# A two-block attention and FFN kernel on one core: another order at the beginnings of three attention passes

## The reference

```
x = x + 0.5 * _L0_ffn_ref(_layernorm(x), ...)      # passes 0 and 1 (DEPTH = 2)
x = x + _L0_attn_ref(_layernorm(x), ...)           # causal linear attention
x = x + 0.5 * _L0_ffn_ref(_layernorm(x), ...)      # passes 2 and 3
x = x + 0.5 * _L1_ffn_ref(...); x = x + _L1_attn_ref(...); x = x + 0.5 * _L1_ffn_ref(...)

# one layer of _L0_ffn_ref
h = shift_token(x); q, k, v = split(h @ wqkv)      # 8 heads of 64
q, k = rotary_xpos(l2norm(q) * qs, l2norm(k) * ksc)
o = local_attention(q, k, v)                       # window 128, looks one block back
x = x + o @ wo
h = layernorm(shift_token(x)) * lg + lb
a, g = split(h @ w1 + b1); x = x + (a * gelu(g)) @ w2 + b2
```

## Time and profile before

| what | value |
|---|---|
| device time, median of 3 runs | 3074.22 us (3072.13 to 3074.41) |
| the profiled execution: its device time, its span | 3073.63 us, 3071.7 us |
| busy share of the span: PE, PE weight load, DVE, ACT, POOL | 95%, 83%, 76%, 57%, 54% |
| shares of the chain that ended last | PE 82%, DVE 7%, issue 4%, POOL 3% |
| mean granted TensorE clock | 0.989 of full speed |
| pass 0, 1 and 3: first attention transpose on PE | 19.06, 612.46 and 2019.63 us |
| second scores (slot 1) on PE | 52.56, 643.17 and 2051.91 us |

### The profile page before, as it was taken

One profiled execution on the slowest core, in us unless ns is written; L12 is line 12 of the kernel. 1 busy time (PEld: TensorE's weight loads), 2 busy tenths in 40 slices (PEclk: granted clock), 3 DMA queues, 4 the chain that ended last, 5 costly groups with the idle time before them and its releaser, 6 DMA issues.

```text
span 3071.7 us, 95309 instructions
## 1 busy us (share of the span) xinstructions
PE 2927.1 (95%) x34258; PEld 2561.2 (83%) x34258; DVE 2340.4 (76%) x6543; ACT 1745.9 (57%) x4596; POOL 1655.8 (54%) x1836
## 2 busy tenths in 40 slices
PE   6999989989999999998999989989999899999899
PEld 5888878878887888887888878878888788888788
DVE  6888777677777787877677777767777788777766
ACT  4777742267777224775777762257777422554345
POOL 7778830078886224334788851057888345227610
PEclk9999999999999999999999999999999999999999
DMA  4211121021111101000211121012111200100001
GB/s 141 71 45 45 45 82 31 24 62 43 42 39 39 44 20 43 12 11 26 64 42 39 39 87 32 24 32 69 41 40 44 62 21 7 28 1 1 1 15 41
DMA packets 178759, 122.62 MB, mean 40 GB/s; under 512 B 27532, under 2 KB 175336, under 8 KB 178024
## 3 DMA queue, kind: packets, MB, share of 16 engines
q1 hardware_dynamic: 177432, 117.77, 14.3%
q10 hardware_dynamic: 1104, 1.90, 0.2%
HBM read 48.29 MB, written 20.98 MB: 23 GB/s over the span
## 4 chain that ended last, share of the span: by engine, by line
PE 82%; DVE 7%; issue 4%; POOL 3%; DMA 1%; ACT 1%; SPq 1%; DVEq 0%; POOLq 0%; ACTq 0%
PE bank L377 7%; PE bank L379 7%; PE bank L378 7%; PE pair_bank L561 6%; PE scores L522 5%; PE scores L377 4%; PE scores L378 4%; PE scores L379 4%; PE bank L492 3%; PE pair_bank L377 2%; PE pair_bank L788 2%; PE pair_bank L787 2%; PE pair_bank L786 2%; PE scores L732 2%; PE scores L731 2%
## 5 line engine op out<-in xcount | busy, mean ns | idle before, releaser
L2736 POOL TENSOR_TENSOR prob<-prob,rsum 128x384 f32<-128x384 f32 x512 | 457.4, 922 | 254.6 <-DVE rsum L1925 254.6
L1261 ACT ACTIVATE prob<-prob,nmax 128x192 f32<-128x192 f32 x1024 | 452.1, 444 | 158.5 <-DVE nmax L1919 158.5
L1463 ACT ACTIVATE gate<-scores,bias 128x512 f32<-128x512 f32 x192 | 132.4, 690 | 511.9 <-PE scores L379 511.9
L2723 POOL TENSOR_TENSOR rn<-ss,mhalf 128x16 f32<-128x16 f32 x128 | 375.3, 2932 | 10.7
L2704 POOL TENSOR_TENSOR rstd<-meanvar,eps 128x4 f32<-128x4 f32 x48 | 11.0, 230 | 624.1 <-DVE meanvar L1850 624.1
L377 PE MATMUL bank<-wqkv_hi,hT_hi 128*128 128x512 f32 x768 | 335.1, 436 | 8.0 <-DVE hT_lo L1858 3.7
L2730 POOL TENSOR_TENSOR qk<-rot_t 128x512 f32<-128x512 f32 x256 | 322.6, 1280 | 19.4 <-DVE ss L1892 12.7
L1919 DVE CUSTOM_DVE_ANT_0 prob<-scores,masks,rn 128x192 f32<-128x192 f32 x768 | 267.5, 414 | 65.6 <-PE scores L522 65.2
L379 PE MATMUL bank<-wqkv_hi,hT_lo 128*128 128x512 f32 x768 | 305.2, 397 | 0.2 <-issue 0.2
L378 PE MATMUL bank<-wqkv_lo,hT_hi 128*128 128x512 f32 x768 | 303.1, 395 | 0.0
L1268 ACT ACTIVATE probT<-scores 128x384 f32<-128x384 f32 x512 | 225.3, 497 | 10.7 <-PE scores L540 10.7
(11 more groups left out here) (347 smaller groups left out, 9530.9 us busy)
## 6 DMA issues: line engine op xcount, KB each, us to landing
Vlo<-V SPq DMA_DIRECT2D x256, 64.0 KB, 2.0
Vhi<-V SPq DMA_DIRECT2D x256, 64.0 KB, 2.0
H<-Y SPq DMA_DIRECT2D x128, 64.0 KB, 1.8
H<-ya SPq DMA_DIRECT2D x128, 64.0 KB, 1.8
yb<-Y SPq DMA_DIRECT2D x128, 64.0 KB, 1.6
HB<-Y SPq DMA_DIRECT2D x32, 256.0 KB, 2.8
HB<-yb SPq DMA_DIRECT2D x32, 256.0 KB, 3.1
raw<-in_L_ffn_wqkv SPq DMA_DIRECT2D x4, 1536.0 KB
```

The costliest lines, as they stand in the source:

```text
L1261: e.activation(pb, pb, ACT.Exp, bias=nm[r][:, x:x + 1], scale=-1.0, accum_out=sums[r][:, x:x + 1]).then_inc(s_acEX[gi], 1)
L2723: e.tensor_tensor(rn[u][:, :], ss[u % 2][:, :], mhalf[:, :], ALU.pow).then_inc(s_plRN, 1)
L2736: e.tensor_tensor(pair, pair, rs[:, 2 * gi:2 * gi + 2].unsqueeze(2).to_broadcast([P, 2, KW]), ALU.mult).then_inc(s_plPN[gi], 1)
```

## The change

The change rewrites the beginning of passes 0, 1 and 3 and gives these passes a first slot with an order of its own (`first_slot`), on PE, ACT, DVE and POOL. Tile 2 is the third tile.

- PE: the transposes of tile 0's q move ahead of `v_(1, 1)`. The waits for POOL's preparations and for the FFN's last Y sums stand behind `v_(1, 1)` instead of ahead of `qk_(1, 1, 0)`. The k projection of tile 2 moves ahead of the transposes of tile 0. The q projection of tile 2 moves behind the first scores.
- ACT: the square of tile 2's q moves from before the first exponentials to behind them; the copies of the turned q of tile 0 and of v of tile 1 change places.
- DVE: the last Y sums (`finish`) move behind `norm_(0, 0, 1)`. The rotation and the sum of tile 2's q move behind the first scores. In the first slot they stand ahead of the second `rs_`, the rotation of tile 2's k and the low part of tile 3's input.
- POOL: in passes 1 and 3 `wo_weights` and the first mask move from ahead of tile 0's adds to behind them (pass 0 had them there). Tile 2's q add moves behind the four `pn_` of the first slot.

```diff
@@ PE, begin and the new first slot
                     ht(2, 2)
+                    qk_(1, 1, 0)
+                    qk_(2, 2, 1)
+                    tr_(0, 0, 1)
+                    tr_(0, 0, 0)
+                    v_(1, 1)
                     e.wait_ge(s_prepB, need['B'] + 4 + OFF)
                     if run:
                         e.wait_ge(s_dvYB, U * GRP * run + OFF)
-                    qk_(1, 1, 0)
-                    tr_(0, 0, 1)
-                    qk_(2, 2, 1)
-                    v_(1, 1)
-                    tr_(0, 0, 0)
+
+                def first_slot():
+                    sc_(0, 0)
+                    ht(3, 3)
                     qk_(2, 2, 0)
+                    v_(2, 2)
+                    pt_(0, 0, 0)
+                    pt_(0, 0, 1)
+                    tr_(1, 1, 0)
+                    qk_(3, 3, 0)
+                    tr_(1, 1, 1)
+                    pt_(0, 0, 2)
+                    pt_(0, 0, 3)
+                    qk_(3, 3, 1)
@@ ACT
                     tr_(0, 0, 1)
+                    tr_(0, 0, 0)
                     v_(1, 1)
-                    tr_(0, 0, 0)
+
+                def first_slot():
+                    qk_(2, 2, 1)
+                    sc_(0, 0, 0)
+                    sc_(0, 0, 1)
                     qk_(2, 2, 0)
+                    ht(3, 3)
+                    v_(2, 2)
+                    pt_(0, 0, 0)
+                    pt_(0, 0, 1)
+                    tr_(1, 1, 0)
+                    qk_(3, 3, 0)
...
@@ DVE
-                    if finish:
-                        finish()
                     qk_(1, 1, 1)
                     ht(2, 2)
                     norm_(0, 0, 1)
+                    if finish:
+                        finish()
                     sum_(1, 1, 1)
                     sum_(1, 1, 0)
                     qk_(1, 1, 0)
...
+                def first_slot():
+                    sc_(0, 0)
+                    rs_(0, 0, 0)
+                    norm_(1, 1, 1)
                     qk_(2, 2, 0)
+                    rs_(0, 0, 1)
+                    qk_(2, 2, 1)
+                    ht(3, 3)
                     sum_(2, 2, 0)
+                    sum_(2, 2, 1)
+                    qk_(3, 3, 0)
+                    sum_(3, 3, 0)
@@ POOL
                     e.memset(V[U - 1][:, :], 0.0).then_inc(s_prepB, 1)
-                    wo_weights()
...
-                if run:
+                if run == DEPTH:
                     mask_of(0)
...
                     add_(0, 0, 0)
-                    if run == 0:
-                        wo_weights()
-                        e.wait_ge(s_raw2, need['raw2'] + OFF)
-                        mask_of(0)
+                    wo_weights()
+                    e.wait_ge(s_raw2, need['raw2'] + OFF)
+                    mask_of(0)
...
+                def first_slot():
+                    add_(1, 1, 1)
+                    for gi in range(NG):
+                        pn_(0, 0, gi)
+                    add_(2, 2, 0)
+                    pow_(2, 2)
```

More of the change, by code:

```diff
@@ L669, in pass_A @@
                 for u in range(U):
-                    slot(u, u)
+                    if u == 0 and run != DEPTH:
+                        first_slot()
+                    else:
+                        slot(u, u)
                     if u < 2:
@@ L1357, in pass_A @@
                     begin()
-                slot(0, 0)
                 if run == DEPTH:
+                    slot(0, 0)
                     linear_tail['yn'](NT - 1)
+                else:
+                    first_slot()
                 for u in range(1, U):
@@ L2038, in pass_A @@
                     e.wait_ge(s_stb, 16 * GRP * ((run + 1) // 2) + OFF)
-                iteration(0)
+                for u in range(U):
+                    if u == 0 and run != DEPTH:
+                        first_slot()
+                    else:
+                        slot(u, u)
+                    extra(0, u)
                 with e.Fori(0, NIT - 2 if run else GRP - 4) as i:
```

## The result

The changed kernel takes 3084.05 us (median of 6 runs, 3082.59 to 3091.99) beside 3074.04 us for the kernel before on the same chip (6 runs, 3070.16 to 3076.29). The ratio is 1.004, 95% interval 1.0029 to 1.0052: slower by 10 us. The forecast was 3077.9 us with a range up to 3081.5, so the time lies outside it, on the slow side.

A forecast was written before the change was run, and what follows sets the result against it. PE's chain of waits (82%) was taken as the bound. Passes 1, 3 and 0 add 1.55 + 1.55 + 0.6 = 3.7 us: profiled 3073.63 becomes 3077.3, on the median 3077.9 us; range 3073.0 to 3081.5.

The forecast's parts named there:

- The order: Beginnings of passes 1, 3 and 0: the new instruction order lengthens them by 1.55, 1.55 and 0.6 us, 3.7 together.
- the held normalisation: DVE, tile 0's k, passes 1 and 3: POOL's add starts first and holds it, so the 1.58 us stays.
- the chain through DVE's rotation: Tile 0's q transposes wait for DVE's rotation of tile 1's q, ending at 628.77; first scores only 0.33 us earlier.
- the exposed table load: ACT ahead of the first exponentials: 0.69 us of the load shows, leaving 0.90 of 1.59 us gained.
- tile 3's q behind its low part: PE, first slot: this projection waits for DVE's low part of its input and comes 1.55 us later.
- The clock: PE in the beginnings: the forecast allowed a fall of the granted clock more or less, 3076 to 3080 us.
- rival 1: PE in the beginnings: clock falls twice in each, four more falls at 1.57 us, +10 us, 3084; chance 0.12.
- The price of a fall: PE in the beginnings: one fall to 1.2 GHz costs 1.57 us, read from pass 3 before.
- 2: DVE, passes 1 and 3: normalisation not held, all behind it 1.1 us earlier, +1.5 us, 3075.7; chance 0.13.
- 3: First slot stays as short as it was, only the earlier reading of scores counts: -5.0 us, 3069.2; chance 0.07.
- 4: ACT, passes 1 and 3: exposed table load costs more, +1.1 us together, sum 4.8 us, 3079.0; chance 0.08.

The follow-up runs named there:

- experiment 5: Changed kernel with 7 spare 32-bit matmuls a pass filling PE's waits ahead of tile 0's q transposes and in the first slot: 3086.89 us (one run).
- experiment 2: Kernel before with ten spare matmuls in PE's first-slot wait for the first probabilities, passes 0, 1 and 3: 3077.38 us, ratio 1.0006.
- experiment 1: Changed kernel with 22 spare 512-column matmuls a pass filling PE's waits ahead of tile 0's q transposes and in the first slot: 3084.77 us, ratio 1.0037.
- experiment 12: Changed kernel with four spare 32-bit matmuls only in the wait ahead of tile 0's q transposes, passes 1 and 3: 3079.77 us, ratio 1.002.
- experiment 3: Changed kernel with v of tile 1 back ahead of tile 0's q transposes on PE and ACT: 3080.62 us, ratio 1.0022.
- 4: Kernel before with only tile 2's q moved into the first slot, on all four engines: 3078.77 us, ratio 1.0008.
- 6: Changed kernel with DVE's last Y sums back ahead of the rotation of tile 1's k: 3073.04 us in a single run.
- 9: Changed kernel with POOL's tile 0 q add waiting for DVE's normalisation of tile 0's k, passes 1 and 3: 3081.81 us, ratio 1.0023.
- 7: Kernel before with only the Y sums moved behind the normalisation, and PE's wait for them behind the beginning: 3077.55 us (one run).
- experiment 8: Kernel before with POOL's tile 0 q add waiting for DVE's normalisation of tile 0's k, passes 1 and 3: 3073.6 us, ratio 0.9998.
- 10: Changed kernel with DVE's last Y sums back ahead of the rotation of tile 1's k, timed over ten runs: 3079.27 us, ratio 1.002.
- 11: Changed kernel with Y sums back in their old place and POOL's tile 0 q add behind DVE's normalisation, passes 1 and 3: 3079.79 us, ratio 1.0013.

## Why the prediction was wrong

**The order: right.** Spare matmuls take the clock out of the comparison. Without falls pass 1 costs +1.51 us (predicted 1.55): first scores 0.27 us earlier (0.33), slot 1.78 us longer. Pass 3 costs 32.22 - 30.69 = +1.53. In pass 0 I took +0.6. There DVE's layer norm sets when the scores are read: 21.34 us from the first transpose after, 21.35 in experiment 5 although its first scores come 1.6 us later. The readings, after first and experiment 5 (first transpose at 18.75) second:

```profile
40.71 0.42 DVE L1951 CUSTOM_DVE_ANT_0 prob<-scores,mask,rn 128x192 f32<-128x192 f32 x1 [0.16 <-issue]
40.10 0.42 DVE L1959 CUSTOM_DVE_ANT_0 prob<-scores,mask,rn 128x192 f32<-128x192 f32 x1 [0.19 <-PE scores L522]
```

So the pass is split at that reading. Without a fall it takes 33.34 us in the new order (experiment 5). In the old one it is an estimate: 23.03 us to the reading (before), and 9.39 from there to the second scores (experiment 2, no fall in that part), 32.42. That is +0.92. Together 3.96 us, where the forecast had 3.7. The reasons stood too: the held normalisation, the chain through DVE's rotation, the exposed table load (in experiment 1 it ends 0.69 us behind the first row minimum, as worked out), tile 3's q behind its low part. In experiment 12 it waits for just that (0.94 us for hT_lo); after, slow transposes put ACT's copy of the turned q last instead.

**The clock: the step that failed.** The prediction let the clock fall once more or less, and gave 0.12 to rival 1, two falls in each beginning. Its case against that rival was "pass 1 had 7.7 us of waits at a clock of 1.00". That sum did not carry over. In pass 1 before the longest wait was 2.55 us and other work stood between the waits; the prediction's own working had a single piece of 3.4 us ahead of tile 0's q transposes (3.33 measured), and three waits of about 1 us with only transposes between them in the slot. Both were followed by a fall in passes 1 and 3 each time that they were left unfilled, and in neither pass when they were filled. Over the profiles without spare matmuls in the slot, the new slot fell in passes 1 and 3 in all 16 cases (after, 3, 4, 6, 9 to 12), the old one in 2 of 6 (before, 7, 8). The result is three falls more than before, five for two.

**The price of a fall: too small.** 1.57 us was taken from the earlier trace rows, and is right for the old slot (1.59, experiment 2). The new ones are split where DVE first reads the scores, since the first fall also slows the scores themselves (2.30 us instead of 1.57). Counted from the first transpose, DVE reads them at 22.14 us in pass 1 and 21.92 in pass 3, and at 19.79 and 19.78 in experiment 1: the first fall costs 2.35 and 2.14 us. From that reading to the second scores it takes 14.34 and 14.42 us, and 12.43 and 12.44 in experiment 1: the second costs 1.91 and 1.98. In pass 0 it costs 35.28 - 33.34 = 1.94. The price is not fixed: in experiment 12 the same fall in the slot cost 2.80 us in pass 1 and 1.57 in pass 3.

**The sum.** Falls after: 2.35 + 1.91 + 2.14 + 1.98 + 1.94 = 10.32 us. Falls before: 1.59 in pass 3 and 33.50 - 32.42 = 1.08 in pass 0, 2.67 us. The difference of 7.65 and the order's 3.96 are the 11.6 us of the three stretches. With 1.6 us less elsewhere this makes the 10.0 of the profiled executions. Rival 1 had +10 as well, from four more falls at 1.57 us (6.3) and an order of 3.7; there were three more, dearer ones. What the rest of the program does from one execution to the next is also more than the microsecond or two that the 3 runs of before let one expect (3072.13 to 3074.41): the two profiles of experiments 6 and 10 differ by 6.5 us there.

**The other rivals.** 2 did not happen (1.76 us). 3 did not: the slot grew in every kernel that has tile 2's q in it. 4 did not: the load took 1.28 us, with its exponential 0.06 us behind.

**What stays open.** What a fall needs in general is not shown. For the second one the runs show that filled waits remove it (1 and 5) and that tile 2's q in the slot is enough for it (4). Ahead of the first scores the clock also fell without the long piece: in pass 3 of experiment 3, and in pass 0 of 2, 4 and 8 behind waits of 2.10, 2.21 and 2.16 us. Why spare matmuls in the slot cost 6 to 12 us elsewhere (1, 2, 5) while four ahead of it cost nothing (12) is not explained. PE's waits for "issue" at L561 add up to 17.1 to 21.2 us in all four kernels with spare matmuls, 12 too, and to 11.0 to 13.7 in the ten without, so they are at most a part of it. No version beat the kernel before; the best, experiment 8, is level with it.

## What to carry over

Where a change rearranges waits on PE, look at the single pieces and at what runs between them, and not only at their sum: a wait that other matmuls used to break up can cost its own length and then half speed behind it. Count each piece that becomes longer than any that the trace shows at full clock as a likely fall, and give its price a range (1.1 to 2.8 us here). One profile of a kernel is one draw: the same wait was followed by a fall in some executions and not in others. And when an edit makes an engine early for something that a later stage must wait for anyway, the gained time comes back as idle time in a new place.

## What the runs showed of the hardware

- At a granted clock of half the speed, 512-column matmuls take 0.63 to 0.80 us instead of 0.39 to 0.51, and four transposes 1.09 instead of 0.63. One fall cost 1.1 to 2.8 us here.
- PE idle for 3.33 or 3.34 us was followed by half clock (4 of 4 such waits, in after and 9; in pass 3 of 9 only from the third matmul of v on). In passes 1 and 3, waits of 1.42 to 1.89 us (6, 10, 11) and 2.34 to 2.36 us (7) ahead of transposes were not. In pass 0, waits of 2.10, 2.16 and 2.21 us were (2, 8, 4) and of 2.12 and 2.14 us were not (7, before). The wait of 3.33 us filled with matmuls was not, in 6 of 6 (1, 5, 12). The Trainium skill (TensorE: Matmul & The Clock Gate, "What's actually happening") calls the throttled clock the default that activity lifts; the pair of the same wait idle and filled agrees with it.
- A DVE instruction with two inputs in SBUF took 1.58 and 1.76 us beside a POOL add that started first, and 0.68 and 0.69 us when the add waited for it (before and after, 8 and 9).
- In the four kernels with spare matmuls PE's "issue" waits at L561 were 17.1 to 21.2 us over the execution, in the ten without 11.0 to 13.7.
- Runs of one program vary here by about 10 us from lowest to highest, so that a single run (3073.04 for what is 3079.27) can mislead by 0.2%.
